# The waits in front of POOL's scatters and gathers in a fused S4D and mixture-of-experts kernel

## The reference

```python
x = x + _layernorm(attn(_layernorm(x)))          # attn: 4 S4D layers
x = x + _layernorm(ffn(_layernorm(x)))

def ffn(x, w1, w2, router_w):                    # E = 8 experts, I = 256
    probs = softmax(x @ router_w.T)
    topk_weights, selected_experts = top_k(probs, 2)
    for e in range(E):
        ew = sum(topk_weights * (selected_experts == e))
        h = x @ w1[e].T
        y = h[:, I:] * silu(h[:, :I]) @ w2[e].T
        out = out + y * ew
```

## Time and profile before

| | |
|---|---|
| runs, us | 1129.48, 1132.31, 1133.68 (median 1132.31) |
| the profiled execution, us | 1128.13 (span 1126.4) |
| busy: PE, PEld, DVE, ACT, POOL | 65%, 54%, 68%, 50%, 45% |
| mean granted clock of TensorE | 0.847 of full speed |
| expert stage, first to last SiLU | 708.3 to 1063.5 |
| POOL's 120 scatters | 635.7 to 827.8, about 1.0 us each |
| POOL's 120 gathers | 829.2 to 1118.2, about 1.0 us each |

### The profile page before, as it was taken

How to read it: one execution, slowest core, us unless ns; L and a number is a source line. 1 busy time by engine, 2 the same in 40 slices (tenths; PEclk the granted TensorE clock), 3 DMA queues, 4 the chain that set the end, 5 groups by cost and what they waited for, 6 DMA issues and landing times.

```text
span 1126.4 us, 25371 instructions
## 1 busy us (share of the span) xinstructions
PE 727.7 (65%) x8523; PEld 610.8 (54%) x8524; DVE 761.7 (68%) x1889; ACT 561.1 (50%) x1197; POOL 509.2 (45%) x704
## 2 busy tenths in 40 slices
PE   0049087895779486967788747668778818926800
PEld 0038086664767386747766536546656707815700
DVE  8987957696669767795759965466556606704797
ACT  7539920394118710592038754335556607704854
POOL 2114234264426543374427667665664271171075
PEclk9999589896989798998889855799999958956955
DMA  7808799927995399909950012113344323322224
GB/s 288 316 5 248 244 385 367 352 98 264 386 347 219 135 374 332 373 10 359 387 235 1 10 65 84 40 48 107 126 120 127 112 56 107 111 69 76 89 78 147
DMA packets 120744, 205.48 MB, mean 182 GB/s; under 512 B 18380, under 2 KB 43480, under 8 KB 119768
## 3 DMA queue, kind: packets, MB, share of 16 engines
q1 hardware_dynamic: 112984, 188.66, 47.4%
q0 software_dynamic: 7680, 15.74, 4.7%
HBM read 167.40 MB, written 36.96 MB: 181 GB/s over the span
## 4 chain that ended last, share of the span: by engine, by line
issue 31%; PE 24%; POOL 20%; DVE 11%; ACT 7%; another core or an unknown queue 5%; DMA 2%; POOLq 1%; SPq 0%; ACTq 0%; DVEq 0%
PE bank L1186 9%; POOL zbuf L612 6%; PE bank L1205 5%; POOL rstd_of L601 4%; POOL toep L685 3%; PE bank L1021 3%; PE bank L999 2%; DVE glu_work L1786 2%; POOL sums L592 1%; DMA toep<-kernels_dram 1%; PE bank L1145 1%; ACT glu_work L958 1%; ACT toep L895 1%; ACT ln_tmp L884 1%
## 5 line engine op out<-in xcount | busy, mean ns | idle before, releaser
L1186 PE MATMUL bank<-toep 128*128 128x256 f16 x1248 | 166.7, 283 | 73.2 <-issue 39.1
L1021 PE MATMUL bank<-zbuf,toep 128*128 128x128 f16 (+3 forms) x3328 | 146.1, 206 | 94.9 <-DVE zbuf L1401 72.3
L1021 PEld LDWEIGHTS bank<-zbuf,toep 128*128 128x128 f16 x3328 | 142.4, 102 | 99.3 <-issue 51.1
L1186 PEld LDWEIGHTS bank<-toep 128*128 (+1 forms) x1248 | 120.3, 101 | 106.1 <-issue 88.9
L612 POOL TENSOR_TENSOR zbuf<-zbuf,w_cur 128x256 f32<-128x256 f32 x120 | 91.2, 761 | 141.0 <-DVE zbuf L1465 141.0
L670 POOL DMA_INDIRECT z_sorted<-toep x120 | 120.0, 1000 | 67.1 <-remote 29.8
L1465 DVE TENSOR_REDUCE zbuf<-bank 128x256 f32<-128x512 f32 x128 | 87.0, 687 | 72.6 <-PE bank L1021 72.6
L1056 PE MATMUL bank<-wo_cur,glu_work 128*128 128x256 f32 x512 | 134.3, 407 | 2.6 <-ACT glu_work L829 2.2
L1786 DVE TENSOR_TENSOR glu_work<-bank,glu_work 128x512 f32<-128x512 f32 x104 | 71.7, 689 | 81.2 <-issue 41.8
L829 ACT ACTIVATE glu_work<-bank,unscale_cur 128x512 f32<-128x512 f32 x64 | 42.8, 668 | 162.9 <-PE bank L1043 162.8
L685 POOL DMA_INDIRECT toep<-y_sorted,toep x64 | 69.9, 1092 | 110.8 <-DMA y_sorted<-toep 91.9
(11 more groups left out here) (269 smaller groups left out, 1500.9 us busy)
## 6 DMA issues: line engine op xcount, KB each, us to landing
toep<-kernels_dram SPq DMA_DIRECT2D x104, 1024.0 KB, 14.0
glu_work<-kernels_dram SPq DMA_DIRECT2D x16, 1024.0 KB, 14.2
toep<-z_sorted SPq DMA_DIRECT2D x88, 128.0 KB
y_sorted<-toep SPq DMA_DIRECT2D x88, 128.0 KB
z_sorted<-ln_tmp SPq DMA_DIRECT2D x3, 3072.0 KB, 23.5
toep_last<-kernels_dram SPq DMA_DIRECT2D x8, 1024.0 KB, 14.1
hres<-in_x SPq DMA_DIRECT2D x1, 4096.0 KB, 13.1
toep<-in_x SPq DMA_DIRECT2D x1, 4096.0 KB, 23.9
```

What stands on the lines that cost most here:

```text
L1021: last = MM(dst[:, d * (B // 4):, :], toep_slot(g)[:, c, d * P:(d + 1) * P, k], z_conv[:, 0:QUADS - d * (B // 4), g * GROUP + c].rearrange ...
L1186: last = MM(out[:, piece % 2 * XP:(piece % 2 + 1) * XP], w1_row[:, pw, bass.ds(e + piece * P, P)], xT_s[:, px * XP:(px + 1) * XP], start=( ...
```

## The change

Each transfer keeps its place in POOL's order and its data. What it waits for changes. The 36 first wait for two quads more (16 at most). After them every transfer belongs to a step: the first of two waits for `s_hid` of that step, the second for `s_yps` of one less. For the scatters and for the gathers of segments 0 and 3 the step follows from the transfer's number with a lead of 1 (`LEAD`), where it was 4. For the gathers of segments 1 and 2 it is counted from the step in which the last tile of the segment is stored.

```diff
+LEAD = 1
...
-            def in_step():
+            def in_step(stored=None):
...
                 d = transfers[0]
                 transfers[0] += 1
                 if d < 36:
                     if d % 3 == 0:
-                        pool.wait_ge(s_z2T, 4 + d // 3)
-                elif d % 2 == 0 and d >= 46:
-                    pool.wait_ge(s_hid, (d - 36) // 2 - 4)
+                        pool.wait_ge(s_z2T, min(6 + d // 3, QUADS))
+                    return
+                if stored is None:
+                    step, second = (d - 36) // 2 - LEAD, d % 2
+                else:
+                    step, second = stored
+                if 0 < step < STEPS:
+                    if second == 0:
+                        pool.wait_ge(s_hid, step)
+                    else:
+                        pool.wait_ge(s_yps, step - 1)
...
                     for t in range(first, first + n):
-                        in_step()
+                        i_g = 2 * (first - SEGMENTS[g][0]) + k * n + t - first
+                        in_step((DENSE_STEPS + FIRSTS[g] + XTS[g] + 2 + i_g // 2, i_g % 2) if 0 < g < SEGS - 1 else None)
```

## The result

| | before | after |
|---|---|---|
| median of the compared runs, us | 1132.99 (1129.48 to 1133.73, 4 runs) | 1079.63 (1077.70 to 1080.37, 4 runs) |
| span of the profiled execution | 1126.4 | 1076.0 |
| mean granted clock | 0.847 | 0.873 |
| first SiLU | 708.34 | 700.93 |
| last SiLU | 1063.51 | 1012.99 |

The ratio of the times is 0.9532, with a 95% interval of 0.9508 to 0.9557. The change saves 53 us; 1078 was forecast.

The account below looks back on a forecast made before the run. No engine's busy time bounds the kernel; POOL's back-to-back transfers hold up TensorE and its reports. Gains 45.6 - 2.9 + 9 = 51.7 us from 1128.1 give 1076, said as 1078 for the median; range 1050 to 1102.

Parts of the forecast that it names:

- The bursts go: Gathers of segments 1 and 2: 76.0 us of bursts go, 32 paired steps cost 30.4, net gain 45.6 us.
- The halves don't separate the pair: Expert steps: despite the second wait transfers stay in pairs, starting behind the second half; step stays 3.19 us.
- the price of a pair: Expert steps: a pair of POOL transfers adds 0.95 us to a free step of 2.24 us.
- LEAD: Scatters and segment 0's gathers: lead 1 instead of 4 makes three more paired steps, 2.9 us lost.
- Scatters before the experts: Before the expert stage: waiting two quads more brings the first SiLU to 699.0; gain 9 us, bounds 0 and 18.
- The fourth scatter: Before the experts: transfer 3 waits for quad 6, done near 642.2, hidden before POOL's last moments with 0.4 us to spare.
- Tail: After the last y tile is stored: POOL is free in both kernels, unchanged at about 56 us.
- the transfers get cheap: Rival, expert steps: a paired step costs 0.5 us instead of 0.95, 38 us more gain, 1040 us; chance 13%.
- The gaps aren't POOL's: Rival, TensorE's gaps: a cause in its own instruction stream merely coincides with the bursts; 1132 us; chance 4%.
- the period of 3.19 us: Paired expert step: two transfers, gaps and TensorE's late report sum as 0.24 + 0.96 + 0.30 + 0.96 + 0.73 us.

Follow-up runs that it names:

- e1: The kernel before with only the gathers of segments 1 and 2 counted from their segment's end, without the second wait; 1090.39 us.
- e2: The changed kernel without its wait for s_yps, so each second transfer goes right behind the first; 1089.24 us.
- f4: The changed kernel with gathers of segments 1 and 2 one behind every step from step 62, leftovers behind the last step; 1074.49 us, one run.
- first two sets: Eight follow-up kernels on the first chip that changed the waits or grouping of POOL's transfers; 1058.82 to 1090.39 us.
- g3: The kernel before, on the second chip, with only the scatters ahead of the experts waiting for two quads more; 990.84 us, ratio 0.9996.
- e4: The changed kernel with gathers of segments 1 and 2 in threes behind every second step; 1072.27 us.

## Why the prediction was right

- *The bursts go.* Forecast: 76.0 us gone and 32 paired steps at 3.19 in their place. Measured: 3.18 and 3.16 us, and the stretches from the 60th to the 76th and from the 83rd to the 99th SiLU fall from 72.0 + 76.3 to 50.8 + 50.5 us, 47.0 saved; some transfers run on into the free steps behind, and from the 60th to the last SiLU 174.8 us become 129.4, 45.4 saved beside a forecast of 45.6. That it comes out so close is partly luck: the first gather can't go before the 61st step, so two of the first 16 steps stay free (2.34 and 2.20 us), the third takes 4.38, and two transfers fall behind the 76th. These nearly even out. e1, with this part alone, saves 43.3 us behind the 60th.
- *The halves don't separate the pair.* Right: 1.27 and 1.90 us apart in the timeline, behind L1216. But I took the second wait for empty, and e2 showed that it isn't: it caps the run of transfers at a segment's opening, worth about 3 us of the 6.7 that e2's steps are longer. The forecast reckoned neither with the long openings nor with what shortens them. And it took the dense steps for pairs, where runs of four go; that they too showed 3.1 us was no support for the price of a pair.
- *LEAD.* Forecast 2.9 us lost. The steps 52 to 60 take 21.4 us instead of 18.1, 3.3 lost, but up to the 60th SiLU together it is 182.7 instead of 180.4, 2.3 lost, and e1, with the waits of the kernel before up to there, takes 182.3. A loss of this size can't be told from what profiles differ by.
- *Scatters before the experts.* Forecast 9 us, from 708.3 to 699.0; measured 7.4 (7.6 from the moments on). The reports of quads 9 and 15 came at 658.68 and 685.10, forecast 658.5 and 684.9, so 8.2 us were gained at the last quad, before any wait for a step. The step that was off is the last: the report behind the burst took 2.2 us, not 1.4, and the burst ended a microsecond later.
- *The fourth scatter.* Forecast hidden, with 0.4 us to spare. It ended at 642.66, and the moments started 0.18 us later than before (642.83 against 642.65). The cover was just used up; the cost can't be seen in the time.
- *Tail.* 62.9 and 63.0 us: unchanged. The sum, 51.7 forecast, is 50.4 in the trace. The 1078 adds to 1076 only half of the 4.2 us by which the median lies higher; with all of it the forecast is 1080.

Of the rivals, "the transfers get cheap" was true of lone ones alone (f4), which this change doesn't make. "The gaps aren't POOL's" is wrong where the time was taken: where POOL's transfers were spaced the gaps closed, in every kernel of the first two sets. But g3 gives it a part of the truth, since POOL's transfers alone don't make the gaps; the chip has to do its share. The traces of the second chip agree with the Trainium skill's rule (SBUF — State Buffer, "SBUF: two separate sides") that a compute operation and a DMA can't slow each other: 346 matmuls in 30 us beside the gathers. On the first chip what the prediction drew from it, that moving the transfers would bring nothing, was wrong: it brought 53 us; no run shows whether the SBUF is where the two meet, so the rule itself is neither shown nor refuted there.

I read the period of 3.19 us as a fixed 0.7 us delay of the report. With four in a run (6.2 us for two steps, against 0.24 + 4 x 0.96 + 3 x 0.30 + 0.73 = 5.7) the formula falls short by half a microsecond: it described the pair, and doesn't carry over to other lengths. Nor does the reading behind it, that the report waits for the last transfer's end: in the burst one came through 11.2 us late with POOL still issuing, and beside f4's lone transfers none was late. The forecast needed only the pair's measured price, which the change left as it was.

## What to carry to other kernels

The "busy" and "issue" shares of the page didn't show this hold-up (31% "issue" before and after); dividing stretches by the count of one instruction per step does, and it priced this change within 2 us. Where POOL's indirect transfers stall TensorE, a pair behind every step was the dear way to spread them: one behind each step was free, three behind every second cost 0.28 us a step, a pair behind each 0.94, and a burst of 32 some 38 us (half of the forecast's 76.0). And take the time of such a change on more than one chip: here it is 4.7% on one and, as an estimate from its parts, nothing on another, where the nearest relative of the first chip's fastest version loses 1.1%.

## What the runs showed of the hardware

- The same kernel took 1129 to 1133 us (medians) on one chip and 992 on another, with equal durations of POOL's instructions; 140 of the 142.7 us between the two profiles lie in stretches where POOL issues indirect transfers, and the eight steps that have none in the kernel before take 18.1 us on both.
- On the first chip matmuls come one or two at a time within a burst, 2.1 us apart in the earlier trace rows and 1.4 us in the last two rows of e4. A run of six gathers makes one step long (7.78 us in e4), one of 32 two steps (13.37 and 25.43 us in the first burst of the kernel before).
- On the first chip a report of TensorE came 11.2 us late in a burst, mostly 2.6 to 3.2 us in steps with pairs before the change, and within 0.1 us beside lone transfers; on the second chip, beside gathers back to back, a first layer's SiLU starts 0.04 us behind it, as in free steps.
- With four transfers per two steps a step takes 3.04 us, with two per step 3.18, with three per two 2.52, with one 2.26.
